# Adjacency products as 64x64x64 pieces, with each graph's result in a PSUM bank of its own

## What is computed

```python
h = relu(layernorm(x))
x = x + attention(h)                  # adj-masked scores, normalised per row
h = relu(layernorm(x))
g = h
for _ in range(3):                    # gated graph network
    a = adj @ g                       # a_in and a_out are the same, both matrices are adj
    z = sigmoid(lin(concat(a, a), w3) + lin(g, u3))
    r = sigmoid(lin(concat(a, a), w4) + lin(g, u3))
    c = tanh(lin(concat(a, a), w5) + lin(r * g, u5))
    g = (1 - z) * g + z * c
x = x + g
```

## Time and profile before

| | |
|---|---|
| median of 3 runs | 916.28 us |
| the profiled execution | 915.86 us |
| its span, first to last instruction | 914.1 us |
| TensorE busy | 899.9 us, 98% |
| VectorE busy | 754.1 us, 83% |
| ScalarE busy | 520.9 us, 57% |
| adjacency products (L552) | 48 groups of 8 |

### The profile page before, as it was taken

How to read it: one execution, slowest core, us unless ns; L and a number is a source line. 1 busy time by engine, 2 the same in 40 slices (tenths; PEclk the granted TensorE clock), 3 DMA queues, 4 the chain that set the end, 5 groups by cost and what they waited for, 6 DMA issues and landing times.

```text
span 914.1 us, 14622 instructions
## 1 busy us (share of the span) xinstructions
PE 899.9 (98%) x4760; PEld 772.9 (85%) x4760; DVE 754.1 (83%) x1513; ACT 520.9 (57%) x892; POOL 107.8 (12%) x161
## 2 busy tenths in 40 slices
PE   8999999999999999999999999999999999999996
PEld 7878888888888888888888888888888888888885
DVE  5877879889788887888978888888879888797665
ACT  5465664656457574665745656456655556555552
POOL 1210102101021010210101101120101201020000
PEclk9999999999999999999999999999999999999999
DMA  6013222623245142441414513154221632224222
GB/s 180 24 50 113 93 93 94 205 69 110 84 125 186 46 138 86 143 161 46 147 60 138 184 69 115 46 163 158 91 92 53 204 110 92 92 102 129 73 66 92
DMA packets 75394, 98.73 MB, mean 108 GB/s; under 512 B 8176, under 2 KB 65776, under 8 KB 75376
## 3 DMA queue, kind: packets, MB, share of 16 engines
q1 hardware_dynamic: 75376, 98.50, 33.0%
HBM read 50.76 MB, written 47.71 MB: 108 GB/s over the span
## 4 chain that ended last, share of the span: by engine, by line
PE 95%; DVE 2%; issue 1%; DMA 1%; ACT 1%; SPq 0%; DVEq 0%
PE gate L410 14%; PE gate L411 14%; PE gate L412 14%; PE cand L412 9%; PE cand L410 9%; PE cand L411 9%; PE fea L552 9%; PE fea L485 3%; PE tok L410 3%; PE tok L411 2%; PE tok L412 2%; PE fea L410 1%; PE fea L412 1%; PE fea L411 1%; DMA x_s<-x 1%
## 5 line engine op out<-in xcount | busy, mean ns | idle before, releaser
L796 ACT ACTIVATE r_s<-gate,b_r 128x512 f32<-128x512 f32 x96 | 65.7, 690 | 126.5 <-PE gate L412 126.5
L1110 DVE TENSOR_TENSOR rh<-r_s,h 128x512 f32<-128x512 f32 x96 | 68.5, 745 | 31.1 <-ACT r_s L796 30.6
L809 ACT ACTIVATE z_s<-gate,b_z 128x512 f32<-128x512 f32 x96 | 64.1, 683 | 51.5 <-PE gate L412 51.5
L712 ACT ACTIVATE h_hi<-h 128x512 fp32r<-128x512 f32 x92 | 56.8, 628 | 39.9 <-DVE h L909 21.9
L1082 DVE SCALAR_TENSOR_TENSOR d_s<-z_s,h 128x512 f32<-128x512 f32 x96 | 63.4, 685 | 18.7 <-ACT z_s L809 18.7
L410 PE MATMUL gate<-h_hi,W_hi_u 128*128 128x512 f32 x192 | 77.9, 406 | 0.2 <-DVE h_lo L909 0.2
L815 ACT ACTIVATE c_s<-cand,b_c 128x512 f32<-128x512 f32 x96 | 64.3, 686 | 23.7 <-PE cand L412 22.4
L355 POOL TENSOR_TENSOR rstd<-vare,minus_half 128x4 f32<-128x4 f32 x32 | 42.0, 1312 | 298.8 <-DVE vare L943 298.8
L410 PE MATMUL gate<-a_hi,W_hi_w 128*128 128x512 f32 x192 | 75.6, 394 | 1.1 <-DVE a_lo L909 1.1
L410 PE MATMUL cand<-rh_hi,W_hi_u 128*128 128x512 f32 x192 | 76.3, 397 | 0.0
L411 PE MATMUL gate<-h_lo,W_hi_u 128*128 128x512 f32 x192 | 75.1, 391 | 0.0
(11 more groups left out here) (147 smaller groups left out, 2220.6 us busy)
## 6 DMA issues: line engine op xcount, KB each, us to landing
h_back<-h_trip SPq DMA_DIRECT2D x216, 128.0 KB, 2.8
h_trip<-h_turned SPq DMA_DIRECT2D x40, 512.0 KB, 2.6
out<-o_s SPq DMA_DIRECT2D x16, 512.0 KB, 4.0
x_s<-x SPq DMA_DIRECT2D x15, 512.0 KB, 4.9
hx_trip<-hx SPq DMA_DIRECT2D x14, 512.0 KB, 3.4
hx_back<-hx_trip SPq DMA_DIRECT2D x56, 128.0 KB, 2.8
h_trip<-h_blk SPq DMA_DIRECT2D x14, 512.0 KB, 3.0
h_trip_last<-h_turned SPq DMA_DIRECT2D x7, 512.0 KB, 3.5
```

Of the source, the lines that this page charges most:

```text
L712: return nc.scalar.activation(dst, src, ACT.Copy)
L796: nc.scalar.activation(r_s[:, c, :], gate[:, c, :], ACT.Sigmoid, bias=b_r[:, c:c + 1]).then_inc(r_ready, 1)
L809: nc.scalar.activation(z_s[:, c, :], gate[:, c, :], ACT.Sigmoid, bias=b_z[:, c:c + 1]).then_inc(z_ready, 1)
L1110: nc.vector.tensor_tensor(rh[:, c, :], r_s[:, c, :], h[s][:, c, :], ALU.mult).then_inc(rh_ready, 1)
```

## The change

Each adjacency matmul of 128x128x128 becomes four of 64x64x64, without the zero blocks of `adjT`: e is the graph's place in its pair (64 of the 128 tokens, partitions 64e to 64e+63 of source and `adjT`), f the half of the feature block (64 weight columns, output partitions 64f to 64f+63). The results of e = 0 go to bank 0 of `fea` and those of e = 1 to bank 1, each bank ordered c, q, token. Before were 8 matmuls for a group, now 32. The group signals `fea_full` by 2 once, at its end, and waits once for both banks. The waits for `t_s` are now tied to an increment of a new semaphore, `sources_seen`, which nobody waits for, one per c (one per group where the source is `h0`).

The rounding and the low part are made by e instead of by c: source is one whole bank, destination the 64-token runs of graph e in both column blocks of `a_hi` and `a_lo`. `reset_gate_a` waits for both e ahead of its first product, since each column block now comes from both. Number, size and order of the ScalarE and VectorE operations stay, as does everything else.

```diff
@@ -184,6 +184,7 @@
             sem("m_full"), sem("w_sum"), sem("w_hi_ready"), sem("w_lo_ready"), sem("bias_ready"))
         tok_full, fea_full, fea_taken = sem("tok_full"), sem("fea_full"), sem("fea_taken")
         tok_taken = sem("tok_taken")
+        sources_seen = sem("sources_seen")
         h_is_turned, h_out, h_in, t_ready = sem("h_is_turned"), sem("h_out"), sem("h_in"), sem("t_ready")
         final_ready = sem("final_ready")
         sq_is_turned, part_ready = sem("sq_is_turned"), sem("part_ready")
@@ -222,6 +223,12 @@
 
         def half(e):
             return slice(e * N, (e + 1) * N)
+
+        def set_columns(t, e):
+            return t[:].rearrange("p c (q e n) -> p c q e n", q=Q, e=2)[:, :, :, e, :]
+
+        def set_bank(e):
+            return fea[:, e, :].rearrange("p (c q n) -> p c q n", c=C, q=Q)
 
         @block.sync
         def _(sp):
@@ -545,13 +552,20 @@
                             last = nc.tensor.transpose(tok[:, q, c * P:(c + 1) * P], h[o][:, c, graph_pair(q)], ident[:])
                     last.then_inc(tok_full, 1)
 
-            def adjacency(c, src, n):
-
-                fea_wait(n, c)
-                for q in range(Q):
-                    last = nc.tensor.matmul(fea[:, c, graph_pair(q)], src[:, q, c * P:(c + 1) * P], adjT[:],
-                                            start=True, stop=True)
-                last.then_inc(fea_full, 1)
+            def adjacency(src, n, t_full=None):
+                fea_wait(n, 1)
+                for c in range(C):
+                    if t_full is not None:
+                        pe.wait_ge(t_ready, t_full + c)
+                    if c == 0 or t_full is not None:
+                        pe.sem_inc(sources_seen, 1)
+                    for q in range(Q):
+                        for f in range(2):
+                            part = slice(c * P + f * N, c * P + (f + 1) * N)
+                            for e in range(2):
+                                last = nc.tensor.matmul(set_bank(e)[half(f), c, q, :], src[half(e), q, part],
+                                                        adjT[half(e), half(e)], start=True, stop=True)
+                last.then_inc(fea_full, 2)
 
             def transpose_new(g, s, dst, full):
 
@@ -578,9 +592,9 @@
                     linear(gate[:, o, :], "u3", o, h_hi[s], h_lo[s], True, False)
 
             def reset_gate_a(w, s, n_a):
-                for c in range(C):
-                    pe.wait_ge(a_hi_ready, 2 * w + (c + 1))
-                    pe.wait_ge(fea_taken, 2 * n_a + (c + 1))
+                pe.wait_ge(a_hi_ready, 2 * w + 2)
+                pe.wait_ge(fea_taken, 2 * n_a + 2)
+                for c in range(C):
                     for o in range(C):
                         last = product(gate[:, o, :], weight("w4", c, o), (a_hi[s][:, c, :], a_lo[s][:, c, :]),
                                        False, c == C - 1)
@@ -643,16 +657,12 @@
                 if k == 5:
                     if new:
                         pe.wait_ge(h0_plain, 2 * i + 1)
-                        adjacency(0, h0[o], use("adj 5"))
-                        adjacency(1, h0[o], use("adj 5"))
+                        adjacency(h0[o], use("adj 5"))
                 elif k == 0:
                     pe.wait_ge(h0_plain, 2 * i)
-                    adjacency(0, h0[o], use("adj 0"))
-                    adjacency(1, h0[o], use("adj 0"))
+                    adjacency(h0[o], use("adj 0"))
                 else:
-                    for c in range(C):
-                        pe.wait_ge(t_ready, 8 * i + 2 * k + (c - 1))
-                        adjacency(c, t_s, use("adj %d" % k))
+                    adjacency(t_s, use("adj %d" % k), 8 * i + 2 * k - 1)
 
 
             pe.wait_ge(const_ready, 1)
@@ -682,8 +692,7 @@
             scores(n("rel 1"), n("q 1"))
             transpose_new(0, 0, cand, turned_full)
             pe.wait_ge(adj_in, 32)
-            adjacency(0, h0[0], n("adj first"))
-            adjacency(1, h0[0], n("adj first"))
+            adjacency(h0[0], n("adj first"))
             reset_gate_h_start()
             norms(1, 0)
             weighted_sum_start(1, n("sum 1"))
@@ -694,8 +703,7 @@
             tok_done(n("sum 1"))
             transpose_new(1, 1, tokT, tok_full)
             candidate_rh(0, 0)
-            adjacency(0, h0[1], n("adj 0"))
-            adjacency(1, h0[1], n("adj 0"))
+            adjacency(h0[1], n("adj 0"))
             tok_done(n("new 0"))
             with pe.Fori(0, PAIRS - 1) as i:
                 for k in (1, 2, 3, 4, 5):
@@ -775,9 +783,9 @@
                     copy(t_s[:, :, c * P:(c + 1) * P].rearrange("p q (b f) -> p q b f", b=BL),
                          h_back[:, :, :, c, :].rearrange("p b q f -> p q b f")).then_inc(t_ready, 1)
 
-            def split_a(s, c, n):
-                fea_wait(n, c)
-                copy(a_hi[s][:, c, :], fea[:, c, :]).then_inc(a_hi_ready, 1)
+            def split_a(s, e, n):
+                fea_wait(n, e)
+                copy(set_columns(a_hi[s], e), set_bank(e)).then_inc(a_hi_ready, 1)
 
             def split_new_start(s, src, full, count):
                 for c in range(C):
@@ -1033,9 +1041,9 @@
                     dve.wait_ge(h_hi_ready, 2 * w + (c + 3))
                     sub(h_lo[o][:, c, :], h[o][:, c, :], h_hi[o][:, c, :]).then_inc(h_lo_ready, 1)
 
-            def split_a(v, s, c):
-                dve.wait_ge(a_hi_ready, 2 * v + (c + 1))
-                sub(a_lo[s][:, c, :], fea[:, c, :], a_hi[s][:, c, :]).then_inc(fea_taken, 1)
+            def split_a(v, s, e):
+                dve.wait_ge(a_hi_ready, 2 * v + (e + 1))
+                sub(set_columns(a_lo[s], e), set_bank(e), set_columns(a_hi[s], e)).then_inc(fea_taken, 1)
 
             def turn_h0(g, s, w):
                 dve.wait_ge(h0_in, 16 * BL * (g - 1))
```

## The result

The changed kernel takes 968.73 us (968.19 to 969.33, four runs) beside 916.49 us for the kernel before: ratio 1.0575, 95% interval 1.0562 to 1.0588, slower by 52 us. The forecast was 941, slower by 25.

A forecast was written before the change was run, and what follows sets the result against it. TensorE was taken as the bound (busy 899.9 of 914.1 us, 95% of the chain). 914.1 + 23.6 for the wait on both low parts + 1.4 for the groups, and 1.8 around it, made 940.9 us; range 932 to 1008.

The forecast's parts named there:

- Partly: Rival: small products overlap only partly, 2.1 to 3.4 us a group; between 948 and 995 us, chance 0.12.
- Small edits: Step on TensorE's waits for t_s, the added increment and the wait for bank fea: 0 us, at most 1.4 us lost.
- waiting lowers the clock: Named way to go wrong: waiting TensorE lowers its granted clock, which stood at full in every slice; no size given.
- The wait for both low parts: Ahead of the a products in reset_gate_a: TensorE waits for the end of low part 1; 19.0 to 28.2 us, taken 23.6.
- The catch-up: When TensorE waits, ScalarE and VectorE lose their backlog, so VectorE's lists after k=0, 1, 3 start earlier; total wait 19.0 us.
- the quiet value of 0.61: Wait in us ahead of the a products in the last windows, which do no attention; used for k=0, 1, 3 in the low case.
- the middle of two cases: Wait total taken as 23.6 us, between 28.2 with today's timing and 19.0 if the other engines lose their backlog.
- The products: Step on the adjacency group: 32 small products take 1.9 us where the 8 large took 1.78; about 0.1 us lost a window.
- the lower bound of 0.89 us: Bound for a group of small products if all four quarters of the array work at once: 16 x 56 ns.
- One after the other: Rival: small products do not overlap, group 3.57 us, +1.79 in each of 48 windows; 994 to 1013 us, chance 0.23.
- fixed price: Rival: each record costs 111 ns whatever its size, 7.1 us a group, +255 us; 1171 us, chance 0.07.
- Faster: Rival: all four quarters at once and no wait on low part 1, if it ends before T0+3.7; 873 us, chance 0.03.

The follow-up runs named there:

- hint: The changed kernel, only TensorE's loop over the rounds announces its closing branch at the top of each iteration; 941.03 us.
- cols: The changed kernel, but rounding and low part made by column block again, each from both banks, and reset_gate_a waiting for one block at a time; 935.77 us.
- cols_hint: The same as cols, with TensorE's loop announced at the top of each iteration; 908.44 us, ratio 0.9913.
- wait_only: The kernel before, with one edit: reset_gate_a waits for both column blocks of a ahead of its first product; 941.31 us.
- early: cols_hint with VectorE's update reordered: low part 0 ahead of the second product and difference, low part 1 ahead of the second turn; 897.61 us.
- double: The kernel before, with two rounds in the body of TensorE's loop: three trips, then the seventh round behind it; 922.16 us, ratio 1.0068.

## Why the prediction was wrong

The time lay inside the range and the sign was right, but the loss is twice the forecast one. It fell among the times of the rival *Partly* (948 to 995 us), by luck: that rival wanted groups of 2.1 to 3.4 us, and they took 1.09.

**The step that failed** is one that the prediction does not have. It counted the new products by their time on the array and never by their number: 288 pairs more in the body of a loop. Under *Small edits* it looked at the waits and the added increment alone, priced them at 0 us, and put the length of the loop's code at nothing without a reason. The runs put this at 27.7 us (changed kernel less hint) and 27.3 us (cols less cols_hint). Over six jumps that is 4.6 us each: 3.3 to 3.8 idle, and 1.2 for the next six products at half clock (6 x (0.43-0.23)), or about 2.3 for the next twelve where the clock stays down for 6.8 us. Those windows grew by 5.5 to 5.8 us and the others by 4.4 to 4.6, of which 0.4 to 0.6 remain in the run hint. With the wait's 26.2 us that makes 54, where the loss is 52.

That waiting lowers the clock the prediction had named as a way to go wrong, with full clock in every slice of the earlier trace rows as the reason not to price it. But a 9 there stands for 90% or more, and hides a stretch of half clock that the kernel before has in start-up, behind 1.53 us idle:

```profile
40.50:43.90 3.40, 3.40 (x15) 3.21 (x16) 2.74 (x9) 0.00 (x0) 2.22 (x3) 0.50 0.02 7
```

In the changed kernel's loop the waits of up to 1.1 us never lowered the clock, those of 3.3 to 3.8 us always did.

The Trainium skill (Runtime: NRT & Kernel Launch, Instruction fetch mechanics) has the rule: a taken branch whose target is no longer held must fetch it before anything is executed. The trace of the changed kernel agrees, and its packets of 1.11 MB over 68 are the 16 KiB blocks named there. The page gives TensorE room for 2048 instructions; the new body has 872 x 2 = 1744 plus its waits. The runs show both: fetched anew at each plain jump back (53 packets between 160 and 850 us), kept when the jump is announced (none). So a count below the page's figure does not tell that a body is kept.

**The wait for both low parts**: right in mechanism and nearly in size. Forecast 19.0 to 28.2, taken 23.6; wait_only measured 26.2. In the runs hint and wait_only idle time stands after k = 0, 1, 3, 5 and in the last part (in the changed kernel, after k = 0, the stretch at the jump takes its place). After k = 2 and 4 the windows grew by 0.00 to 0.09 us, but not for the reason given: since the group is shorter, TensorE comes sooner and idles there too, for 0.17 to 0.25 us. The catch-up came as said: low part 1 ends at T0+5.08 after k = 1 where it had ended at 5.53. So the quiet value of 0.61 should have been the whole answer, but the windows after k = 1 and 3 grew by 0.83 and 0.89: the first product after an idle stretch is dearer (0.50, and the next starts 0.34 instead of 0.23 later), 0.13 us with those behind it, and 0.09 us are lost ahead of the next group of small products. That the run hint, without the jumps, took the forecast 941 us is luck: the forecast was the middle of two cases, while the lower one held and costs came on top that it did not have.

**The products**: the size was wrong, harmlessly. Forecast 1.9 us, measured 1.09 from the group's start to the next product. The step at fault is the claim that two records of a product must lie behind one another and so no more than two products side by side. Four records ran at a time, where that claim allows two, as in the lower bound of 0.89 us: 16 steps of 58 ns are 0.93 us. The Trainium skill's rule of starts about 4 ns apart (TensorE: Matmul & The Clock Gate, Packing small matmuls) would have led there; here they are 6 to 7. Of the 0.77 us that 0.93 would save against the 1.70 of before, the windows after k = 2 and 4 got 0.47 in the run cols_hint. The rest goes at the two ends: the next product starts 0.15 to 0.19 us after the group's last record, and the first record starts 0.32 us after the product before it, where the large ones have 0.23. The Trainium skill's other rule (TensorEngine Tiling (Array Packing), Key Properties), that changing the mode drains TensorE, would explain both; no run here shows the cause.

**The rivals.** *One after the other* and *fixed price* fell at the first look at the group. *Faster* had named its point of decision, low part 1 before T0+3.7, and it was at 5.1. The runs cols_hint and early show that this case was real once the a products wait for low part 0 only and that is ready at T0+3.2.

**The small edits in the waits for t_s** cost nothing that a window shows: after k = 2 and 4 0.6 and 0.1 us in all.

## What to carry to other kernels

Count instructions as well as time when a change goes into a loop: 288 more pairs in a body cost 4.6 us at every jump back, and announcing the branch in the loop's header gave 27 us back. When the trace puts an idle stretch down to an engine, look whether it comes once per trip of the loop; here the releaser that it named had been done for 0.9 us. And before making a group of products shorter, find what the engine will wait for next: here the gain of 0.5 us a window came in full only when the wait behind it was split by column block again and the low part moved two places up in VectorE's list, with the announced loop together 897.6 us against 916.0.

## What the runs showed of the hardware

- 64x64x64 fp32 products in four quarters of the array: 64 records in 1.16 us, against 16 records of 128x128x128 in 1.95 us for the same result. Their order matters: 2.69 us if four in a row use the same quarter.
- With a plain loop, a body of 872 pairs is fetched anew each round (68 packets of code) and one of 584 is not (10); six jumps cost 27 us. With the closing branch announced, the body of 872 is not fetched anew either (15 packets, none between 160 and 850 us).
- An increment of a semaphore on TensorE is no free filler: 96 of them made a window about 4 us longer.
- Half the granted clock, for 3.4 or 6.8 us, followed each of the six idle stretches of 3.3 to 3.8 us. In between the length does not decide by itself: in the run double the clock stayed at full behind 2.04 us idle and fell at 2.28, and in the changed kernel it stayed at full behind 2.69 us in start-up. Behind the idle stretch of 1.02 us after k = 1 it stayed at full:

```profile
314.00:317.00 3.00, 2.60 (x11) 2.16 (x12) 1.55 (x3) 0.21 (x1) 0.00 (x0) 1.00 0.43 175
```
